# A spare block of zeroed rows instead of clamped gather indices in a gated cross-attention and mixture-of-experts kernel

## The reference

```python
x = x + tanh(g_xattn[0]) * xattn(layernorm(x), ctx, mask)
x = x + tanh(g_ffn[0]) * ffn(layernorm(x), w_router, w_gate, w_up, w_down)
# xattn: softmax(q @ ctx.T / sqrt(512), masked) @ ctx; zero for a sequence whose mask is all off
# ffn:   probs = softmax(xt @ w_router.T); the two largest, normalised, are the weights comb
#        out = sum over the 2 experts of comb * (silu(xt @ w_gate.T) * (xt @ w_up.T)) @ w_down.T
```

## Time and profile before

| | us |
|---|---|
| median of 3 runs | 296.83 |
| lowest and highest | 296.04 and 298.39 |
| the profiled execution, whole | 296.83 |
| its span, first to last instruction | 295.0 |
| first gather issued by GpSimd | 133.59 |
| last scatter-add issued by GpSimd | 286.66 |

### The profile page before, as it was taken

The page is one execution under the profiler, slowest core; times in us unless marked ns, Lnnn a source line. Parts: engine busy times, 40 slices in busy tenths (PEclk is TensorE's granted clock), DMA queues, the critical chain, the costliest instruction groups (busy, mean ns, idle before and its releaser), DMA issues.

```text
span 295.0 us, 5554 instructions
## 1 busy us (share of the span) xinstructions
PE 254.8 (86%) x1501; PEld 215.4 (73%) x1501; DVE 171.2 (58%) x650; ACT 147.0 (50%) x310; POOL 164.4 (56%) x151
## 2 busy tenths in 40 slices
PE   1799997988989975457999999999999999999940
PEld 1677775665767745346899999889989999999920
DVE  4477778977896888982344444444444444444420
ACT  3469855566667446121255555434445544444430
POOL 1256657444455536416156686884766748748370
PEclk9999999999999998557899999999999999999995
DMA  7996878888899525404347577775895967859584
GB/s 223 372 376 182 295 230 314 269 269 268 255 309 399 184 80 199 118 2 122 96 72 136 88 144 139 116 143 109 158 170 104 154 133 128 159 86 171 109 123 59
DMA packets 25950, 52.08 MB, mean 177 GB/s; under 512 B 5248, under 2 KB 5376, under 8 KB 25920
## 3 DMA queue, kind: packets, MB, share of 16 engines
q0 software_dynamic: 8304, 19.83, 37.1%
q1 hardware_dynamic: 17616, 31.89, 32.5%
HBM read 33.81 MB, written 17.89 MB: 175 GB/s over the span
## 4 chain that ended last, share of the span: by engine, by line
PE 58%; DMA 16%; DVE 12%; SPq 4%; issue 4%; ACT 2%; POOL 1%; ACTq 0%; POOLq 0%; DVEq 0%
PE S L1064 9%; PE S L1068 9%; PE S L1065 9%; DMA out<-X 8%; PE A L1054 6%; DMA x2s<-Y 5%; PE S L930 3%; PE PO L941 3%; DVE TB L716 2%; DMA X<-in_x 2%; SPq L306 2%; PE PL L1087 1%; PE PO L1087 1%; PE PO L1089 1%; PE PO L1088 1%
## 5 line engine op out<-in xcount | busy, mean ns | idle before, releaser
L441 POOL DMA_INDIRECT out<-YT,IXI x36 | 56.8, 1578 | 42.4 <-issue 20.2
L1064 PE MATMUL S<-WGh,XTh 128*128 x144 | 51.8, 360 | 1.4 <-ACT XTh L536 1.4
L1065 PE MATMUL S<-WGl,XTh 128*128 x144 | 48.8, 339 | 0.0
L415 POOL DMA_INDIRECT XG<-x2s,IXG x39 | 38.6, 989 | 18.0 <-issue 10.1
L870 DVE TENSOR_TENSOR H<-SG,S 128x192 f32<-128x192 f32 x36 | 12.7, 354 | 48.0 <-ACT SG L543 40.5
L385 POOL TENSOR_TENSOR WGl<-WGl,WGh 128x512 fp32r<-128x512 f32 x24 | 30.6, 1280 | 16.6 <-ACT WGh L500 16.5
L543 ACT ACTIVATE SG<-S 128x192 f32<-128x192 f32 x36 | 11.9, 331 | 50.2 <-PE S L1068 41.2
L376 POOL TENSOR_TENSOR rs<-mv,CS 128x1 f32<-128x1 f32 x32 | 17.7, 553 | 31.9 <-DVE mv L610 31.9
L863 DVE TENSOR_TENSOR XTl<-A,XTh 128x512 fp32r<-128x512 f32 x37 | 25.6, 692 | 13.9 <-ACT XTh L536 13.9
L941 PE MATMUL PO<-CX,PT 128*128 128x512 f32 x64 | 31.1, 609 | 1.3 <-DVE X L650 1.3
L1068 PE MATMUL S<-WGh,XTl 128*128 x144 | 31.5, 342 | 0.0
(11 more groups left out here) (153 smaller groups left out, 540.4 us busy)
## 6 DMA issues: line engine op xcount, KB each, us to landing
WGl<-in_wgu SPq DMA_DIRECT2D x24, 256.0 KB, 4.8
X<-in_x SPq DMA_DIRECT2D x16, 256.0 KB, 4.0
CT<-in_ctxt SPq DMA_DIRECT2D x8, 512.0 KB, 5.9
CX<-in_ctxn SPq DMA_DIRECT2D x8, 512.0 KB, 5.2
out<-X SPq DMA_DIRECT2D x16, 256.0 KB, 4.6
x2s<-Y SPq DMA_DIRECT2D x16, 256.0 KB, 4.8
WD1l<-in_wd SPq DMA_DIRECT2D x8, 256.0 KB, 5.2
WS<-in_wd SPq DMA_DIRECT2D x8, 256.0 KB, 4.2
```

The source lines that it names most:

```text
L415: pool.indirect_dma_start(out=XG[:, j % NX, :], out_offset=None, in_=x2s, in_offset=bass.IndirectOffsetOnAxis(ap=IXG[:, j:j + 1], axis=0))\
L441: pool.indirect_dma_start(out=out, out_offset=bass.IndirectOffsetOnAxis(ap=IXI[:, j:j + 1], axis=0), in_=YT[:, j % NB, :], in_offset=None, ...
L1064: pe.matmul(o, XTh[:, j % 2, c, :], WGh[:, bass.ds(e, 1), c, :], start=(c == 0), stop=False)
L1065: pe.matmul(o, XTh[:, j % 2, c, :], WGl[:, bass.ds(e, 1), c, :], start=False, stop=False)
```

## The change

The scratch tensor `x2s` gets the same 2688 rows as `out`. At the start GpSimd clears a 128 x 520 piece of `Y2` (called Z), and SyncE, after `loadx(6)` and ahead of its step loop, stores it ten times: to the five spare blocks of `x2s` and to the five of `out`. ScalarE's first `x2ln`, which overwrites Y2, and GpSimd's first gather wait for these stores. The index table `IXG` and its instruction go; the gathers use `IXI`, so padding slots read the cleared rows. The closing waits move from SyncE's stream to the end of GpSimd's.

```diff
-    x2s = nc.dram_tensor("x2s", [T, DW], fp32, kind="Internal").ap()
+    x2s = nc.dram_tensor("x2s", [ROWS, DW], fp32, kind="Internal").ap()
...
-        IXG = sb("IXG", [128, NTP], i32)
...
+        Z = Y2[:].rearrange("p i d -> p (i d)")[:, 0:DW]
...
@@ block.sync, behind the loads of tiles 4 to 6
+            sp.wait_ge(s_z, 1)
+            for i in range(NB):
+                r = slice(T + 128 * i, T + 128 * i + 128)
+                sp.dma_start(x2s[r, :], Z).then_inc(s_zd, 16)
+                sp.dma_start(out[r, :], Z[:, 0:D]).then_inc(s_zd, 16)
             for s in range(STEPS + 2):
...
-            live = tiles_of(sp)
-            for i in range(NB):
-                sp.wait_ge(s_add[i], 16 * ((NF + NB - 1 - i) // NB))
-            for j in range(NF, NT):
-                with lives(sp, live, j):
-                    sp.wait_ge(s_add[j % NB], 16 * (j // NB + 1))
-            for j in range(NT - NX, NT):
-                with lives(sp, live, j - NX):
-                    sp.wait_ge(s_g[j % NX], 16 * (j // NX + 1))
...
@@ block.gpsimd
+            pool.memset(Z, 0.0).then_inc(s_z, 1)
             pool.wait_ge(s_c, 16)
...
-            pool.wait_ge(s_ixg, 1)
+            pool.wait_ge(s_ixi, 1)
+            pool.wait_ge(s_zd, 32 * NB)
...
-                                        in_offset=bass.IndirectOffsetOnAxis(ap=IXG[:, j:j + 1], axis=0))\
+                                        in_offset=bass.IndirectOffsetOnAxis(ap=IXI[:, j:j + 1], axis=0))\
...
             pool.wait_ge(s_tn, 1)
-            pool.wait_ge(s_ixi, 1)
...
+            landed(NF)
+            for j in range(NF, NT):
+                with lives(pool, live, j):
+                    pool.wait_ge(s_add[j % NB], 16 * (j // NB + 1))
+            for j in range(NT - NX, NT):
+                with lives(pool, live, j - NX):
+                    pool.wait_ge(s_g[j % NX], 16 * (j // NX + 1))
@@ block.scalar, x2ln
+                if k == 0:
+                    act.wait_ge(s_zd, 32 * NB)
@@ block.vector
-            dve.tensor_scalar(IXG[:, :], PC[:, 0:NTP], float(T), float(T - 1), ALU.add, ALU.min).then_inc(s_ixg, 1)
```

More of the change, by code:

```diff
@@ L97, in flamingo @@
         MS = sb("MS", [128, 8, 2, E], bf16)
+        IXI = sb("IXI", [128, NTP], i32)
         ER = sb("ER", [1, NTP], i32)
-        IXI = sb("IXI", [128, NTP], i32)
-        IXG = sb("IXG", [128, NTP], i32)
         TF = sb("TF", [1, 39])
@@ L180, in flamingo @@
         s_ws = [sem(f"s_ws{i}") for i in range(NST)]
+        s_z = sem("s_z")
+        s_zd = sem("s_zd")
         s_d = sem("s_d")
@@ L226, in flamingo @@
         s_ixp = sem("s_ixp")
-        s_ixg = sem("s_ixg")
         s_ixi = sem("s_ixi")
```

## The result

The changed kernel takes 309.72 us (median of 4 runs, 306.84 to 310.30) against 297.61 us (4 runs, 296.04 to 299.61). The ratio is 1.036 with a 95% interval of 1.031 to 1.042. The change makes the kernel slower, as forecast, but by twice the 5.5 us that the forecast had and beyond its range.

What follows compares the result with a forecast made beforehand. The prediction took SyncE's loop of `out` landings and reloads to pace attention, and TensorE at 3.92 us per tile the feed-forward stage. 5.0 + 0.2 + 0.3 = 5.5 us on 296.8 gave 302.3 us, range 299.0 to 306.0.

Steps and rivals of the forecast that it cites:

- The zero stores: Attention stage: ten stores ahead in the DMA queue push the loads behind them back by 6.8 us, 9 at most.
- the half clock: TensorE after its stall: the PV matmuls run at 1.2 GHz, making the compute path about 2 us later still.
- the slack of 1.7 us: Attention stage: the compute path could lose 1.7 us of its delay, since SyncE's loop sets the pace.
- the stage's term of 5.0: Attention stage: 5.0 us later in all, between 4.6 by SyncE's loop and 5.4 by the compute path.
- what SyncE's loop was to be given back: Attention stage: `out(1)` lands 3.5 to 4.5 us after issue, not 6.2, leaving SyncE's loop 4.0 to 5.0 us late.
- The index table: VectorE before the first gather: the gathers wait for IXI instead of IXG, +0.2 us on the chain.
- Nothing of the change touches that loop's work.: Feed-forward stage: its loop of tiles stays at 3.92 us per tile.
- The closing waits: End of the kernel: moving them from SyncE to GpSimd costs -0.3 to +1.1 us, taken as +0.3.
- The tail: Rival at the kernel's end: dearer GpSimd branches and emptying its queue add 2 us more, 304 us; chance 0.08.
- Hidden: Rival in the attention stage: the zeros fill DMA gaps and SyncE's loop catches up, 297.3 us; chance 0.14.
- More is lost: Rival in the attention stage: stores a third slower (9 us) and half clock over more steps, 305.5 us; chance 0.18.

Runs made afterwards that it cites:

- e13: The changed kernel with 42 instead of 32 constant matmuls before the feed-forward stage's first transposes and 8 more before its first gate matmuls; 307.55 us, ratio 1.038.
- e6: The changed kernel with the ten zero stores moved to SyncE's step 20 and the closing waits back on SyncE; 297.60 us, ratio 1.003.
- e3: The changed kernel with the same ten zero stores issued late, in SyncE's step 20 (about 117 us); 301.91 us, ratio 1.016.
- e12: The kernel before with 16 never-taken branches added at the end of GpSimd's stream; 298.00 us, ratio 1.011 (0.984 to 1.038).
- e11: The kernel before with SyncE's closing waits for the gathers put ahead of those for the scatter-adds; 295.65 us, no interval could be given.

## Why the prediction was right in its sign and wrong in its size

- **The zero stores.** Right in all steps but one: 0.66 us per store (0.68), unit 1 at 23.7 (24.1), ScalarE's wait 5.94 (5.9), `out(0)` landed at 29.8 (30.0), the new waits free, the memset over at 1.25 us. The TensorE stall was 5.05 us (5.1), and the half clock on the PV matmuls cost 1.9 (2). The layer norm of tile 3 was 7.1 us late, which is 5.1 + 2, that of tile 8 5.5 and the last one 5.42: that fits the slack of 1.7 us against SyncE's loop, though no run isolates it, and the stage's term of 5.0 measured 5.4. The step that was wrong is what SyncE's loop was to be given back: `out(1)` was to land 3.5 to 4.5 us after its issue at 32.0 and took 5.7, so it came 6.3 us later than before and not 4.0 to 5.0. That the 5.0 came so near is in part luck.
- **The index table.** +0.23 for +0.2.
- **"Nothing of the change touches that loop's work."** This step put the stage at nothing; it measured 2.5 us in the two profiles. 1.39 of them are TensorE's clock, which was 0.50 through the whole first tile; by the other profiles that may be scatter, and it isn't shown to come from the change (e13). The other 1.1 us are in the loop, and 0.9 of them go with the new index over all profiles (e6). Of these, 0.6 lie in the tiles from 13 to 21, where each profile shows a few tiles that take up to 5.0 us for 3.92: the excess there is 0.9 to 1.7 us in the five kernels with `IXG` and 1.7 to 2.1 in the eleven with `IXI`. So the gathers were a part of the loop that the change did touch. By which way the index slows these tiles stays open.
- **The closing waits: the step that failed.** The prediction put them at -0.3 to +1.1 and took +0.3; they cost 4.0. It priced the instructions well: they take 1.08 us on GpSimd, where SyncE took 1.06. It took SyncE's last wait of 2.2 us for a handshake that starts when SyncE arrives, and so the same for whoever comes last. It was a wait for GpSimd's DRAIN. Before the change the DRAIN began at 286.92, beside the last scatter-add, and only the 3.12 us behind the landing showed. The change put it behind the waits for the landing, and all 6.20 us of it stand at the end: 12.35 = 4.84 + 1.08 + 6.20 + 0.23, for 8.36.
- **The rivals.** "The tail" named the right place with +2 for a price and 0.08 for a chance, on the ground that nothing in the profile showed such a cost. The profile had the cost in it: the DRAIN of 7.86 us at line 42, open until 0.24 us before the end, beside 3.5 us without a byte moved. "Hidden" fell at once: `out(1)` landed at 37.8, not before 32. "More is lost" has the nearest time of all, 305.5, for the wrong reason: stores alone run at 398 GB/s (e3); its 9 us for the stores would have been 9.7 by its own 273 GB/s.

## What to carry to other kernels

A store at the head of a queue that everything is loaded through costs its full transfer time to whoever waits at the tail, even if nobody waits for the store; the same bytes cost at most about 1 us some 100 us later. Before a wait is moved between engines at the end of a kernel, look up what each engine's last instruction is and how long it lasts, also where the profile doesn't count it as work: let the engine with the long DRAIN (here GpSimd) reach it early, and let another wait for the last landing. And where a stage starts with a pause, look at TensorE's granted clock over its first tile in more than one profile: 18 added matmuls went with 1.4 us less there than in the kernel before, but another kernel had as little without them.

## What the runs showed of the hardware that I had not expected

- GpSimd's DRAIN at the end of its stream lasts 6.20 us if it starts behind the last landing (eight profiles) or 2.13 us ahead of it (e12). If it starts 4.5 us or more ahead of it, it ends 3.12 us behind the landing (seven profiles). On SyncE the same instruction takes 0.01 us and on VectorE 0.02 to 0.11.
- In SyncE's profile this shows as a wait for TensorE's queue, `SPq L42 <- PEq L42`, 2.2 us before, 2.7 in e11 and 3.5 in e12: the name of the releaser there isn't the engine that is late.
- An untaken branch on GpSimd costs 0.15 us, and it can run beside a scatter-add that the engine is still busy with (e12).
- Stores of 2048- and 2080-byte rows alone run at 398 GB/s (e3), like the loads.
